# Three of four query and key tiles of a quarter leave VectorE for ScalarE and two strided DMAs each

## The chip, the cores and the metric

One core of a Trainium2 chip runs the whole program in one launch. The metric is the device time of one execution in microseconds, here over three runs. All data is fp32.

## The reference

Three stages follow each other on 64 images of 3x96x96 and 64 texts of 77x256:

```python
h = tokenizer(x)                       # conv 14x14, window attention, class token: 5 tokens of 256 per image
h = concatenate([h, txt], axis=1)      # 64 x 82 x 256
h = h + attention(layernorm(h))        # 16 heads of 16, sine/cosine relative bias
h = h + experts(layernorm(h))          # 8 experts, low rank 64, top 2, gelu
# attention:
#   q, k, v = split(ln(x) @ w_qkv + b_qkv)
#   p = softmax(q @ k.T * 16**-0.5 + rel_bias[i - j])
#   out = (p @ v) @ w_out + b_out
```

## The kernel before

The tokenizer runs first. After it the attention runs as a pipeline written out by hand, one block b (one image, T = 82 tokens) per period, b = 0 to 63. Each engine has its own list of steps for a period, and semaphores join them. GpSimd normalises rows, adds the residual and scatters rows for the experts. In the last blocks the experts' work begins, and it goes on after the loop.

In a period TensorE does, in this order: `scores(b)` (L1443, 32 small matmuls into the four banks `psS`), `weigh(b-2)` (L1464), `turn(b-1, 0)` (L1452, a transpose of the probabilities), where due `xT` (L1409, a transpose of 128 token rows) and `val` (L1430, their values), `turn(b-1, 1)`, where due `project` (L1476, the output projection), `turn(b-1, 2)`, one projection `qk` (L1418), a late step of the tokenizer while there are any, and `turn(b-1, 3)`. All but the scores write into a ring of four banks, `psQ`, in the order of a list `uses`; a use waits until the use four places before it has been read.

Queries and keys are made by quarters of 4 blocks (QT = 328 columns). Quarter q has four tiles: j = 0 and 1 are halves of the queries, j = 2 and 3 halves of the keys. `qk(q, j)` is computed in the period with (b + 1) // 4 + 1 = q and (b + 1) % 4 = j, so tile 0 in period 4k + 3, tiles 1 to 3 in the three periods that follow, and the quarter is used from two periods after tile 3. The tiles go to `qT` and `kT`, two views of `qk_space`, double-buffered by q % 2. Each tile is held twice, for a = 0 and 1. In copy a the partitions of parity a hold the queries (or keys) of 16 columns each; the other partitions hold sine and cosine rows, which carry the relative bias through the same matmul and are equal in every quarter. `scores(b)` waits for tile 3 of its quarter and for both halves of the softmax shift of the block before, since `psS` is single.

VectorE does per period: `shift(b, 0)` and `shift(b, 1)` (each a maximum, L1846, and a subtraction, L1848), in even periods between them `invert` (L1863, the reciprocal of the softmax sums), then statistics for token rows, `read_qk` (L1834: two instructions per tile, `copy = bank * own + add`, one for each a), late tokenizer steps, and in odd periods `divide` (L1874).

ScalarE does `copy_sums` (L1665), four `copy_probT` (L1685), two exponentials (L1677), the evictions `copy_xT`, `copy_val`, `copy_project`, and after the fourth `copy_probT` for 16 row tiles a `split` (L1693).

SP issues nearly all DMAs from one queue. In even periods: `pack` (L1147, after the gathered sums have landed), `send_shares` (L1155, after the reciprocal), `load_values` (L1179), values and output stores, `spread_shares` (L1164, two DMAs, after the shares have landed in DRAM), then `load(b)` (tokens or expert weights). In odd periods `gather_den` (L1142) comes first, after `copy_sums`. `divide` waits for the spread.

Of the kernel before, what the change touches and what calls it, by code (L numbers as in the profile page):

```python
# [35 lines left out]
NEARLY = 2  # L36
QLEAD = 2
# [19 lines left out]
def tokenizer_block(nc, ctx, S, I, R, A, L, big, pout, cout, ident_all, banks):  # L57
    NN = NTOK // 128 * TOPK
    HB = NB // 2
    GROUPS = ((0, 1), (1, 2), (2, 4), (4, 9), (9, 13), (13, 18))  # L60

# [37 lines left out]
    gbq_row = sb("gbq_row", [128, C])  # L99
    pj_row = sb("pj_row", [128, C]); gpj_row = sb("gpj_row", [HB, C])  # L100
# [32 lines left out]
    def sync(sp):  # L133
        sp.dma_start(patches[:, 0, 0:QLEAD, :], I["patches"][:, 0, 0:QLEAD, :]).then_inc(S["lead_in"], 16)
        for k, (lo, hi) in enumerate(GROUPS):
            if k == 2:
                sp.dma_start(ei[:], I["ff_expert_indices"]).then_inc(S["r_in"], 16)
                sp.dma_start(ew[:], I["ff_expert_weights"]).then_inc(S["r_in"], 16)
                sp.dma_start(steps[:], I["steps"]).then_inc(S["r_in"], 16)
                sp.dma_start(upper[:], I["upper"]).then_inc(S["r_in"], 16)  # L140
                sp.dma_start(keep[:], I["keep"]).then_inc(S["r_in"], 16)
            if k == 3:
                sp.dma_start(ident_all[:], I["ident"]).then_inc(S["ident_in"], 16)
                sp.dma_start(cols[:], I["cols"]).then_inc(S["ident_in"], 16)
                sp.dma_start(cls[:], row(I["class_emb"], 128)).then_inc(S["ident_in"], 16)
                sp.dma_start(entry[:], I["entry"]).then_inc(S["r_entry"], 16)
                sp.dma_start(R["list"], I["unfilled"]).then_inc(S["r_entry"], 16)
            if k == 4:
                sp.dma_start(wq[:], I["la_wq"].rearrange("(c p) n -> p c n", p=128)).then_inc(S["law_in"], 16)
                sp.dma_start(wkv[:], I["la_wkv"].rearrange("(c p) n -> p c n", p=128)).then_inc(S["law_in"], 16)  # L150
            if k == 0:
                sp.dma_start(patches[:, 0, QLEAD:5, :], I["patches"][:, 0, QLEAD:5, :]).then_inc(S["img_in0"], 16)
            else:
                sp.dma_start(patches[:, lo:hi, :, :], I["patches"][:, lo:hi, :, :]).then_inc(S["img_in%d" % k], 16)
# [104 lines left out]
    def tensor(te):  # L259
# [5 lines left out]
        def conv(n):  # L265

            if n == 0:
                te.wait_ge(S["ones_set"], 1)
                keep_busy(PS8[0], 9)
                te.wait_ge(S["conv_lead_in"], 16)  # L270
                te.wait_ge(S["lead_in"], 16)
            for k, (lo, hi) in enumerate(GROUPS):
                if n == lo and n > 0:
                    te.wait_ge(S["img_in%d" % k], 16)
            if n >= 2:
                te.wait_ge(S["pe_ready"], n - 1)
            if n == 9:
                te.wait_ge(S["v_read"], NW)
            for q in range(5):
                if n == 0 and q == QLEAD:  # L280
                    te.wait_ge(S["conv_in"], 16)
                    te.wait_ge(S["img_in0"], 16)
                mm = te.matmul(PS8[n % 2][:, 0:C], patches[:, n, q, :], cwT[:, q, :], start=(q == 0), stop=(q == 4))  # L283
            mm.then_inc(S["conv_done"], 1)
# [324 lines left out]
    def vector(v):  # L609
# [252 lines left out]
        for n in range(11, 22):  # L862
# [16 lines left out]
            if n == 15:  # L879
# [36 lines left out]
    return (sync, gpsimd, tensor, scalar, vector), {"early": early, "cwT": cwT, "wq": wq, "wkv": wkv, "gwq": gwq}  # L916
# [32 lines left out]
def attention_space(sb):  # L949
# [5 lines left out]
         "wrel": sb("wrel", [128, 2, 2, 2]), "own": sb("own", [128, 2]), "ownq": sb("ownq", [128, 2]), "bown": sb("bown", [128, 2, 4]),  # L955
# [13 lines left out]
def attention_and_experts(nc, ctx, S, I, R, A, L, W, H, pc, ident_all, out, banks, old):  # L969
# [48 lines left out]
    to_act = ("xT", "val", "project")  # L1018
    by_act = {use: 1 + sum(u[0] in to_act for u in uses[:k]) for k, use in enumerate(uses) if use[0] in to_act}
    by_dve = {use: 1 + sum(u[0] == "qk" for u in uses[:k]) for k, use in enumerate(uses) if use[0] == "qk"}  # L1020
# [9 lines left out]
    mx = sb("mx", [T, 2, 2, 4])  # L1030
    prob_all = sb("prob", [128, 2 * HG * 4 * T])
# [45 lines left out]
    texp = R["tile_expert"]  # L1077

# [18 lines left out]
    def sync(sp):  # L1097
# [68 lines left out]

        def send_values(n):
# [20 lines left out]
        for b in range(-1, NB):  # L1188
# [13 lines left out]
            if b >= 4 and b % 2 == 0:  # L1202
                spread_shares(b // 2 - 2)
            load(b)
# [28 lines left out]
        for n in range(0, NX, 2):  # L1233
            sp.dma_start(yg_two(n), rows[:, n:n + 2, :, :]).then_inc(S["yg_in%d" % (n // 2)], 16)
# [134 lines left out]
    def tensor(te):  # L1369
        def free(use):  # L1370

            k = place[use]
            if k >= RING:
# [3 lines left out]
                elif before[0] == "qk":  # L1377
# [263 lines left out]
    def scalar(act):  # L1641
# [9 lines left out]

        def copy_val(n):
# [103 lines left out]
        for b in range(NB):  # L1756
# [20 lines left out]
            if b >= 1:  # L1777
                copy_probT(b - 1, 3)
            for n in projected(b - 5):
# [27 lines left out]
        for n in range(NX):  # L1807
            if n % 2 == 0:
                act.wait_ge(S["yg_in%d" % (n // 2)], 16)
# [3 lines left out]
    def vector(v):  # L1813
# [148 lines left out]
        for b in range(NB):  # L1962
# [13 lines left out]
            if (b + 1) // 4 + 1 < NQ:  # L1976
# [28 lines left out]
        for n in range(0, NX, 2):  # L2005
            v.wait_ge(S["yg_in%d" % (n // 2)], 16)
# [181 lines left out]
```

## Time and profile before

| | us |
|---|---|
| median of 3 runs (598.92 to 599.81) | 599.6 |
| the profiled execution, its own time | 596.89 |
| its span, first to last instruction | 595.0 |
| PE busy over the span | 545.7 |
| VectorE (DVE) busy | 477.2 |
| ScalarE (ACT) busy | 367.1 |
| GpSimd (POOL) busy | 314.5 |

The span is the profile's own window, some 2 us shorter than the time of the same execution. Matmuls are pipelined and their ends are modelled, so a busy TensorE is not yet one that has no time to give. The time before an instruction is told as idle time of its engine, with what released it. A chain row says what the end of the program was waiting for at that moment, so a duration there is the part that counts, without overlaps.

### The profile page before, as it was taken

To read this page: it belongs to the slowest core of one execution; us is meant where nothing else is said; L and a number is where in the kernel's file an instruction comes from. 1 tells how busy PE (TensorE), PEld (TensorE's weight loads), DVE (VectorE), ACT (ScalarE), POOL (GpSimd) and SP (SyncE) were. 2 spreads that over 40 slices of the span, in tenths; PEclk is the share of its full clock that TensorE was granted. 3 is DMA by queue.
4 is the path that set the end of the run, shared out by engine and by line. 5 is a ranking of instruction groups with operands and counts; after the bars stand their busy time and mean duration, and the time that the engine had idled before them with its cause. 6 is when DMAs were issued, how large, how long until landed. Compare 5 with 4: busy or idle time off the path is not lost.

```text
span 595.0 us, 20410 instructions
## 1 busy us (share of the span) xinstructions
PE 545.7 (92%) x7904; PEld 456.3 (77%) x7904; DVE 477.2 (80%) x967; ACT 367.1 (62%) x793; POOL 314.5 (53%) x401
## 2 busy tenths in 40 slices
PE   9999989989999999999999999999998799999940
PEld 7788867767788778877888788888886678888830
DVE  3666868898999899999999889998887756666617
ACT  1232234156676677777777677677778667777724
POOL 1577773436746688888888524443121244444430
PEclk9999999989999999999999999999999999999975
DMA  8999301422332334666666644333254354545349
GB/s 280 399 326 333 103 10 43 137 76 82 103 87 87 115 125 134 186 200 199 206 206 194 188 137 148 96 119 124 87 144 139 84 131 107 114 117 114 68 140 327
DMA packets 78185, 89.49 MB, mean 150 GB/s; under 512 B 33550, under 2 KB 58638, under 8 KB 77580
## 3 DMA queue, kind: packets, MB, share of 16 engines
q1 hardware_dynamic: 73340, 78.20, 42.9%
q0 software_dynamic: 4464, 9.35, 5.1%
q8 instruction: 64, 1.05, 0.8%
q10 hardware_dynamic: 288, 0.66, 0.3%
q14 instruction: 29, 0.24, 0.1%
HBM read 48.82 MB, written 36.29 MB: 143 GB/s over the span
## 4 chain that ended last, share of the span: by engine, by line
PE 60%; DVE 20%; issue 8%; DMA 5%; ACT 4%; SPq 1%; POOL 1%; DVEq 0%; POOLq 0%; ACTq 0%
PE banks L1452 8%; PE banks L1418 7%; PE banks L1562 7%; PE banks L1464 6%; DVE mx L1846 6%; PE banks L1577 6%; PE banks L1430 5%; PE banks L1476 4%; PE banks L283 3%; PE banks L1443 3%; DVE prob L1848 3%; DVE qk_space L1834 2%; PE banks L323 2%; ACT probT L1685 2%; PE banks L1547 2%
## 5 line engine op out<-in xcount | busy, mean ns | idle before, releaser
L1685 ACT ACTIVATE probT<-banks 82x328 f32<-82x328 f32 x256 | 109.1, 434 | 9.6 <-PE banks L1452 9.3
L1848 DVE TENSOR_TENSOR prob<-banks,mx 82x656 f32<-82x656 f32 x128 | 107.1, 837 | 4.4
L1452 PE MATMUL banks<-ident_all,prob 82*82 82x82 f32 x1024 | 109.6, 237 | 1.1 <-ACT early L1665 0.9
L1452 PEld LDWEIGHTS banks<-ident_all,prob 82*82 82x82 f32 x1024 | 88.1, 120 | 28.2 <-issue 6.7
L1846 DVE TENSOR_REDUCE mx<-banks 82x8 f32<-82x656 f32 x128 | 104.3, 815 | 5.2 <-PE banks L1443 4.0
L1677 ACT ACTIVATE prob<-prob 82x656 f32<-82x656 f32 x128 | 95.5, 746 | 15.8 <-DVE prob L1848 15.1
L1418 PE MATMUL banks<-hT,wqkv 128*128 128x328 f32 (+10 forms) x320 | 80.6, 385 | 0.0
L1296 POOL TENSOR_TENSOR big<-big,gwq 128x256 f32<-128x256 f32 x41 | 30.2, 738 | 88.0 <-ACT gwq L1672 87.5
L1357 POOL DMA_INDIRECT entry_rows<-cwT,slot_entry x39 | 39.7, 1018 | 63.1 <-ACT cwT L1730 57.3
L1665 ACT ACTIVATE early<-banks 128x328 f32<-128x328 f32 x64 | 28.5, 445 | 56.8 <-PE banks L1464 43.8
L1443 PE MATMUL banks<-qk_space 32*82 32x82 f32 x2048 | 53.0, 240 | 7.4 <-DVE prob L1848 5.7
L1892 DVE COPY qk_space<-ex_weights 64x640 f32 x78 | 39.4, 505 | 25.0 <-PE banks L1590 23.8
L1464 PE MATMUL banks<-probT,vv 82*32 82x82 f32 x2048 | 50.1, 238 | 7.5 <-ACT probT L1685 6.5
L1418 PEld LDWEIGHTS banks<-hT,wqkv 128*128 128x128 f32 x320 | 50.3, 191 | 7.6
L1443 PEld LDWEIGHTS banks<-qk_space 32*82 32x82 f32 x2048 | 43.8, 147 | 16.0 <-issue 8.9
L1721 ACT ACTIVATE hT<-banks 128x1024 f32<-128x1024 f32 (+1 forms) x40 | 38.1, 1000 | 21.3 <-PE banks L1562 21.3
L1464 PEld LDWEIGHTS banks<-probT,vv 82*32 82x32 f32 x2048 | 37.8, 110 | 15.5 <-ACT probT L1685 12.1
L1283 POOL TENSOR_SCALAR xh<-big,a_mv,a_rst 128x256 f32<-128x256 f32 x35 | 44.3, 1266 | 6.3 <-PE banks L1409 2.6
L1430 PE MATMUL banks<-wqkv,hT 128*128 128x256 f32 x164 | 43.7, 390 | 0.0
L1476 PE MATMUL banks<-wout,wkv 128*128 128x256 f32 x164 | 43.6, 390 | 0.0
L283 PE MATMUL banks<-cwT,big 128*128 128x256 f32 x180 | 40.5, 381 | 1.8 <-DMA big<-in_patches 1.3
L1562 PE MATMUL banks<-wq,qk_space 64*128 64x128 f32 x624 | 41.1, 278 | 1.1 <-issue 1.1
(275 smaller groups left out, 1011.3 us busy)
## 6 DMA issues: line engine op xcount, KB each, us to landing
vv<-value_rows SPq DMA_DIRECT2D x57, 192.0 KB
value_rows<-vs SPq DMA_DIRECT2D x41, 256.0 KB, 2.9
share<-shares SPq DMA_DIRECT2D x64, 82.0 KB
slot_rows<-xh SPq DMA_DIRECT2D x1, 4992.0 KB, 33.0
fused_rows<-in_txt SPq DMA_DIRECT2D x1, 4928.0 KB
big<-in_patches SPq DMA_DIRECT2D x2, 1600.0 KB, 12.3
out<-big SPq DMA_DIRECT2D x25, 128.0 KB
big<-entry_rows SPq DMA_DIRECT2D x6, 512.0 KB, 6.5
```

The lines of the kernel that those rows point to most:

```text
L283: mm = te.matmul(PS8[n % 2][:, 0:C], patches[:, n, q, :], cwT[:, q, :], start=(q == 0), stop=(q == 4))
L1418: mm = te.matmul(bank(("qk", 4 * q + j))[:, lo:lo + size], wqkv[:, c, 128 * j:128 * j + 128], hT[:, c, a:a + size], start=(c == 0), stop=( ...
L1430: mm = te.matmul(bank(("val", n))[:, 0:C], hT[:, c, a:a + 128], wv[:, c, :], start=(c == 0), stop=(c == 1))
L1443: mm = te.matmul(psS[0:T, g, s:s + T], qT[rows, par, a, t, cols], kT[rows, par, a, t, cols], start=True, stop=True)
L1452: mm = te.transpose(bank(("turn", 4 * b + g))[0:T, s * T:s * T + T], prob[:, b % 2, g, s, :], ident_all[0:T, 0:T])
L1464: mm = te.matmul(bank(("weigh", b))[32 * g:32 * g + 32, lo:lo + T], vv[0:T, b % 4, 8 * t + 2 * g + a, :], probT[:, b % 2, g, 2 * t + a, :] ...
L1476: mm = te.matmul(bank(("project", n))[:, 0:C], attT[:, c, a:a + 128], wout[:, c, :], start=(c == 0), stop=(c == 1))
L1562: mm = te.matmul(psH[:, f // 4, h, f % 4 * 128:f % 4 * 128 + 128], wb[rows, p % 2, f * 128:f * 128 + 128], t1T[rows, p % 2, :], start=True ...
L1677: act.activation(prob[:, b % 2, 2 * half:2 * half + 2, :, :], prob[:, b % 2, 2 * half:2 * half + 2, :, :], ACT.Exp).then_inc(S["prob_ready ...
L1685: act.activation(probT[:, b % 2, g, :, :].rearrange("p s t -> p (s t)"), bank(("turn", 4 * b + g))[0:T, 0:4 * T], ACT.Copy).then_inc(S["pr ...
L1846: v.tensor_reduce(mx[:, half, :, :], s4, X, ALU.max).then_inc(S["max_ready"], 1)
L1848: v.tensor_tensor(prob[:, b % 2, 2 * half:2 * half + 2, :, :], s4, mx[:, half, :, :].unsqueeze(3).to_broadcast([T, 2, 4, T]), ALU.subtract ...
```

## The change

Quarters 0 and 1 stay as they are. From quarter 2 (`QMOVED`) on, tiles 0, 1 and 2 are evicted by ScalarE: one activation of 128x328 with the bias and the scale, into a plain row buffer. SP then places it by two DMAs per tile, each from the 64 partitions of one parity to the same partitions of copy a. The constant partitions of the copies keep what VectorE wrote there for quarters 0 and 1. Tile 3 stays with VectorE. The eviction stands after `copy_probT(b-1, 3)` in ScalarE's list; the placement stands in the next period of SP's list, after `spread_shares` and ahead of `load`. Scores wait for the six placements of their quarter as well. The row buffers lie in tensors of the tokenizer (`red`, `wg1`, `past`), and a few semaphores are shared and renamed, which changes no wait.

```diff
+                v.tensor_scalar(A["qkb"][:, 0:2], cols[:, 20:22], float(HD) ** -0.5, None, ALU.mult)
+                v.tensor_copy(A["qkb"][:, 2:4], cols[:, 22:24])
...
+    QMOVED = 2
+
+    def to_act(use):
+        return use[0] in ("xT", "val", "project") or (use[0] == "qk" and use[1] >= 4 * QMOVED and use[1] % 4 < 3)
...
+    def moved(b):
+        q = (b + 1) // 4 + 1
+        return [(q, (b + 1) % 4)] if ("qk", 4 * q + (b + 1) % 4) in by_act else []
...
+    rows_qk = [old["red"][:].rearrange("p r c -> p (r c)")[:, 0:QT], old["wg1"][:].rearrange("p r c -> p (r c)")[:, 0:QT],
+               old["past"][:].rearrange("p j e -> p (j e)")[:, 0:QT]]
...
+        def send_qk(q, j):
+
+            sp.wait_ge(S["psQ_act"], by_act["qk", 4 * q + j])
+            if j == 0:
+                sp.wait_ge(S["scores_done"], 4 * (q - 1))
+            rows, t = qT if j < 2 else kT, j % 2
+            for a in range(2):
+                sp.dma_start(rows[a:128:2, q % 2, a, t, :], rows_qk[j][a:128:2, :]).then_inc(S["qk_sent%d" % (q % 2)], 16)
+
...
+            for q, j in moved(b - 1):
+                send_qk(q, j)
             load(b)
...
         def scores(b):
 
             te.wait_ge(S["psQ_dve"], by_dve["qk", 4 * (b // 4) + 3])
+            if b // 4 >= QMOVED:
+                te.wait_ge(S["qk_sent%d" % (b // 4 % 2)], 16 * 6 * (b // 8))
...
+        def copy_qk(q, j):
+
+            act.wait_ge(S["qk_done"], 4 * q + j + 1)
+            if j == 0 and q > QMOVED:
+                act.wait_ge(S["qk_sent%d" % ((q - 1) % 2)], 16 * 6 * ((q - 1) // 2))
+            act.activation(rows_qk[j], bank(("qk", 4 * q + j))[:, 0:QT], ACT.Identity, bias=A["qkb"][:, j:j + 1],
+                           scale=float(HD) ** -0.5 if j < 2 else 1.0).then_inc(S["psQ_act"], 1)
...
             if b >= 1:
                 copy_probT(b - 1, 3)
+            for q, j in moved(b):
+                copy_qk(q, j)
...
-            if (b + 1) // 4 + 1 < NQ:
+            if (b + 1) // 4 + 1 < NQ and not moved(b):
                 read_qk((b + 1) // 4 + 1, (b + 1) % 4)
```

## Rows read from the trace of the kernel before

**Rows 1.** Windows: busy us (instructions) per engine, granted clock, DMA share, GB/s

```profile
core 0: us, PE busy (x) PEld busy (x) DVE busy (x) ACT busy (x) POOL busy (x), PEclk, DMA share, GB/s
135.05:440.44 305.39, 297.53 (x5158) 246.26 (x5158) 284.52 (x513) 220.98 (x517) 192.57 (x254) 1.00 0.46 140
265.10:340.57 75.47, 73.54 (x1284) 60.77 (x1283) 70.85 (x129) 57.40 (x134) 63.39 (x82) 1.00 0.65 200
```

**Rows 2.** The page: the chain that ended last, by engine

```profile
PE 60%; DVE 20%; issue 8%; DMA 5%; ACT 4%; SPq 1%; POOL 1%; DVEq 0%; POOLq 0%; ACTq 0%
```

**Rows 3.** The chain in order of time, 240 to 275: start, us, what

```profile
248.81 0.76 PE banks L1443 x32
249.57 0.73 PE banks L1464 x32
250.30 0.41 PE banks L1452 x4
250.71 0.22 PE banks L1409 x2
250.93 0.87 PE banks L1430 x4
...
252.08 0.90 PE banks L1476 x4
...
253.27 1.16 PE banks L1418 x4
...
257.76 0.40 DVE den L1863
```

**Rows 4.** TensorE's groups, 135.04 to 440.43: count, busy, mean ns, idle before

```profile
L1464 PE MATMUL banks<-probT,vv 82*32 82x82 f32 x1792 | 43.9, 238 | 4.1 <-ACT probT L1685 3.2 <-DVE qk_space L1834 0.3
L1430 PE MATMUL banks<-wqkv,hT 128*128 128x256 f32 x144 | 37.4, 382 | 0.0
L1476 PE MATMUL banks<-wout,wkv 128*128 128x256 f32 x132 | 35.3, 390 | 0.0
L1409 PE MATMUL banks<-ident_all,xh 128*128 128x128 f32 x66 | 12.7, 272 | 0.0
```

**Rows 5.** VectorE's groups, 135.04 to 440.43

```profile
L1846 DVE TENSOR_REDUCE mx<-banks 82x8 f32<-82x656 f32 x112 | 91.2, 814 | 1.6 <-PE banks L1443 0.5 <-issue 0.2
L1834 DVE SCALAR_TENSOR_TENSOR qk_space<-banks,own,kadd 128x328 f32<-128x328 f32 x57 | 29.0, 550 | 7.6 <-PE banks L1418 7.5
L1834 DVE SCALAR_TENSOR_TENSOR qk_space<-banks,ownq,qadd 128x328 f32<-128x328 f32 x56 | 28.4, 549 | 5.4 <-PE banks L1418 5.1
```

**Rows 6.** ScalarE's sums copy, 135.04 to 440.43

```profile
L1665 ACT ACTIVATE early<-banks 128x328 f32<-128x328 f32 x56 | 25.0, 446 | 50.1 <-PE banks L1464 39.5 <-DVE wkv L1874 9.3 <-issue 1.3
```

**Rows 7.** Timeline of TensorE: start, us, instruction

```profile
297.38 0.83 PE L1443 MATMUL banks<-qk_space 32*82 32x82 f32 x32
...
361.51 0.83 PE L1443 MATMUL banks<-qk_space 32*82 32x82 f32 x32
```

**Rows 8.** Timeline of SP's queue: start, us on the queue, DMA

```profile
292.76 1.17 SPq L1164 DMA_DIRECT2D share<-shares  x2
294.47 0.56 SPq L1142 DMA_DIRECT2D den<-early  x1
...
299.28 0.53 SPq L1147 DMA_DIRECT2D early<-early  x1
...
325.16 1.16 SPq L1164 DMA_DIRECT2D share<-shares  x2
...
356.93 1.15 SPq L1164 DMA_DIRECT2D share<-shares  x2
```

**Rows 9.** DMA issues, 250 to 300, then 350 to 400: KB, median us to landing

```profile
early<-early SPq DMA_DIRECT2D x5, 82.0 KB, 4.3
...
early<-early SPq DMA_DIRECT2D x5, 82.0 KB, 2.5
```

**Rows 10.** Timeline of VectorE: a division that waited for its spread

```profile
331.19 0.50 DVE L1874 TENSOR_TENSOR wkv<-early,share 128x328 f32<-128x328 f32 x1 [0.70 <-DMA share<-shares]
```

**Rows 11.** Timeline of VectorE in the tokenizer

```profile
94.29 0.22 DVE L887 TENSOR_SCALAR bown<-cols,ownq 128x2 f32<-128x2 f32 x1
94.42 0.22 DVE L888 TENSOR_SCALAR bown<-cols,own 128x2 f32<-128x2 f32 x1
```

More of the change, by code:

```diff
@@ L36 @@
 NEARLY = 2
+GROUPS = ((0, 1), (1, 2), (2, 4), (4, 9), (9, 13), (13, 18))
 QLEAD = 2
@@ L59, in tokenizer_block @@
     HB = NB // 2
-    GROUPS = ((0, 1), (1, 2), (2, 4), (4, 9), (9, 13), (13, 18))
     items = []
@@ L98, in tokenizer_block @@
     bq_row = early[:, 1024:1024 + C]
-    gbq_row = sb("gbq_row", [128, C])
-    pj_row = sb("pj_row", [128, C]); gpj_row = sb("gpj_row", [HB, C])
+    bias_rows = sb("bias_rows", [128, 2, C])
+    gbq_row, pj_row = (bias_rows[:, k, :] for k in range(2))
+    gpj_row = sb("gpj_row", [HB, C])
     cls = sb("cls", [128, C])
@@ L914, in vector @@
             read_quarter(k)
-    return (sync, gpsimd, tensor, scalar, vector), {"early": early, "cwT": cwT, "wq": wq, "wkv": wkv, "gwq": gwq}
+    return (sync, gpsimd, tensor, scalar, vector), {"early": early, "cwT": cwT, "wq": wq, "wkv": wkv, "gwq": gwq, "red": red, "wg1": wg1, "past": past, "bias_rows": bias_rows}
 LATE = ("agg", "aggT", "loutT", "lout", "wpj", "wmod", "gwkv", "gwpj", "gv", "mod_row", "gbv_row", "cls_row", "bkv_row", "xn", "xT", "qv",
@@ L1017, in attention_and_experts, with to_dve @@
     place = {use: k for k, use in enumerate(uses)}
-    to_act = ("xT", "val", "project")
-    by_act = {use: 1 + sum(u[0] in to_act for u in uses[:k]) for k, use in enumerate(uses) if use[0] in to_act}
-    by_dve = {use: 1 + sum(u[0] == "qk" for u in uses[:k]) for k, use in enumerate(uses) if use[0] == "qk"}
+    QMOVED = 2
+    def to_act(use):
+        return use[0] in ("xT", "val", "project") or (use[0] == "qk" and use[1] >= 4 * QMOVED and use[1] % 4 < 3)
+    def to_dve(use):
+        return use[0] == "qk" and not to_act(use)
+    by_act = {use: 1 + sum(to_act(u) for u in uses[:k]) for k, use in enumerate(uses) if to_act(use)}
+    by_dve = {use: 1 + sum(to_dve(u) for u in uses[:k]) for k, use in enumerate(uses) if to_dve(use)}
+    def moved(b):
+        q = (b + 1) // 4 + 1
+        return [(q, (b + 1) % 4)] if ("qk", 4 * q + (b + 1) % 4) in by_act else []
     def sb(name, shape, dt=F32):
@@ L1077, in attention_and_experts, with rows_in @@
     texp = R["tile_expert"]
+    def rows_in(k):
+        return 16 + 16 * (k < len(GROUPS))
     def yg(n, k):
@@ L1233, in sync @@
         for n in range(0, NX, 2):
-            sp.dma_start(yg_two(n), rows[:, n:n + 2, :, :]).then_inc(S["yg_in%d" % (n // 2)], 16)
+            sp.dma_start(yg_two(n), rows[:, n:n + 2, :, :]).then_inc(S["piece_in%d" % (n // 2)], 16)
         for n in range(0, NX, 2):
@@ L1376, in free @@
                     te.wait_ge(S["sums_copied"], before[1] + 1)
-                elif before[0] == "qk":
+                elif before in by_dve:
                     te.wait_ge(S["psQ_dve"], by_dve[before])
```

14 lines of the change are left out of this document (7 added, 7 removed).

## The prediction

> **What bounds the kernel now.** I read the stage table first [rows 1]. The change acts on the blocks b = 3 to 57, in the stretch from 135.05 to 440.44 us, which starts and ends with a group of scores and holds 56 periods in 305.4 us. There TensorE is busy for 297.5 us, VectorE for 284.5, ScalarE for 221.0, at full granted clock and with the DMA engines 46% busy. Two engines near the top: the question is which of them sets the period. The chain of waits over the whole run [rows 2] gives 60% to PE and 20% to DVE, so both do, in turn. Seen in order of time [rows 3], a period is normally TensorE's own list: scores 0.76, weighing 0.73, four turns 0.41 and three times 0.28 (such a turn is what lies between the pieces at 252.08 and 253.27), the query or key projection 1.16, and where they are due a token turn 0.22, values 0.87, the output projection 0.90. Where VectorE comes late, the chain passes through its work instead, as in the reciprocal of the denominators at 257.76.
>
> How much do these latenesses cost? I price TensorE's list for the 56 periods [rows 3, 4]. The fixed part is 2.72 + 1.15 = 3.87, times 56 = 216.7 us. L1430 x144 is 36 value tiles at 0.87 = 31.3, L1476 x132 is 33 projections at 0.90 = 29.7, L1409 x66 is 33 token turns at 0.22 = 7.3. Twenty projections split at the ring's end cost 0.17 more each, 3.4, and the tokenizer's late matmuls are seven blocks of the size of a value tile, 0.87 each = 6.1, and a few small ones, 6.2 together. Sum 294.6. The stretch takes 305.4, so 10.8 us are not TensorE's own work. That is the most a lighter VectorE can give; the busy time it saves is far larger and mostly worthless.
>
> **The change part by part.** *VectorE.* Three of four tiles of quarters 2 to 15 leave it: 42 tiles, 84 instructions of 0.55 us [rows 5], 46 us of busy time before overlap. Its load falls from 93% to about 78% of the stretch, under TensorE's 97%. Scores to scores the fixed chain is the scores' 0.8, two maxima of 0.81 and two subtractions of about the same [rows 5], in even periods the reciprocal of 0.4 [rows 3] between them: 4.2 to 4.7 us with hand-overs, below TensorE's lightest period of 3.87 + 0.90 = 4.77. So late starts of VectorE should vanish. Not all of the 10.8 us: TensorE waits 3.2 us before L1464 for ScalarE's probabilities [rows 4], and most of these waits come in even periods, after the reciprocal and also where VectorE had been idle. I leave 3.3 us standing. Gain 7.5 us, bounds 5 and 10.8.
>
> *ScalarE.* It gets 42 activations of 128x328 from a bank. L1665 is that shape and takes 0.446 us [rows 6]; 42 x 0.446 = 19 us. The Trainium skill, "ScalarE: Activation LUTs", section "What ACT_TABLE_LOAD costs", gives about 93 ns more for a bias that is a pointer; no row here shows this form on this shape, and it would make 23 us. The new copy stands after the fourth probability copy and before the sums copy, L1665, which idles 50.1 us before its 56 runs, 39.5 of them for TensorE's weighing [rows 6]: 0.7 us each time, more than the 0.45. In the sixteen periods where the split copy stands there too, the cover is about used up. The bank is wanted again only four uses later, after the next weighing and turn. Cost 0; with no cover it is 19 us.
>
> *SP and the DMAs.* 84 placements, each from 64 partitions to 64 alternate ones, 82 KB. The pack L1147 is the same in kind and size: 0.53 us on SP's queue [rows 8], landing in 2.5 us where the queue is quiet, in 4.3 us in the 250 to 300 us window [rows 9]. The 7 MB are no burden as bytes. The moment counts. The third tile's pair goes out in the even period 4k+2, behind SP's spread L1164, which waits for the shares' round trip, and the scores of period 4k+4 need it. Quiet quarter: spread 356.93 plus 1.15, second placement from 358.7, plus 2.5 lands at 361.2; scores are due at 361.51 [rows 7, 8]. It fits by 0.3. Loaded quarter: spread 292.76 plus 1.17, second placement from 294.55, plus 4.3 is 298.85; due at 297.38 [rows 7, 8]. 1.5 us late, or 0.3 early with the quiet landing. Queued behind this wait on TensorE are the scores and all that follows, so the wait is paid in full. Four quarters, every fourth period from 276 to 341, lie in the loaded stretch from 265.10 to 340.57, which has 65% DMA share [rows 1]. Bounds 0 and 1.5 us each there, 0 and 0.5 for the other ten; I take 0.9 and 0, that is 3.6 us (0 to 11), nearer to the loaded landing because the spread itself needed about 6.0 us there (SP issues at 325.16, the division ends its wait for it at 331.19) [rows 8, 10].
>
> The Trainium skill, "DMA: Bandwidth & Descriptors", section "Anatomy of one DMA", gives (for the GpSimd path) about 2.0 us and the bytes over 436 GB/s: an estimate of 2.2 us for 82 KB. The quiet row is near it, the loaded row is not, and by the page nothing would be late and the forecast 3.6 us lower. The measurement decides.
>
> Second, SP itself. The placements take 1.1 us of its queue in three periods of four. In even periods they stand before the next block's loads and before the gather of the denominators L1142, which then waits its turn: L1142 starts at 294.47 and its pack, which needs it landed, at 299.28 [rows 8]. The reciprocal, which needs it too, is due after that period's scores, first maximum and first subtraction: 297.38 [rows 7] plus 0.83, 0.81 and about 0.83, at 299.9. The slack there is 0.6 us; delayed by 1.1, it comes 0.5 late, between the two halves of the softmax. Eight gathers in the loaded stretch by 0.5 are 4 us, the upper bound; most even periods have more on TensorE's list than VectorE's 4.7, which hides it: I take 0.7 us in all, lower bound 0. The spread is not preceded by a placement in its own period.
>
> *TensorE.* No matmul changes. Scores get one more wait, 52 times. Weighing, at 249.57, stands behind three waits and starts as the scores end (248.81 plus 0.76) [rows 3]: a wait that is already met costs nothing that shows, and I take 0. I bound it by 0.04 us, a few times the rounding of these pieces: 2 us in all. *Front.* Two more tiny VectorE operations beside the four of L887 and L888, of 0.22 us each and partly overlapping [rows 11], in a stretch where VectorE's row of work leads to the class and patch rows that the first token loads wait for: 0.25 us, bounds 0 and 0.44. Merged tensors, renamed and shared semaphores: nothing issued, nothing waited for longer. GpSimd: nothing.
>
> Sum: 7.5 - 3.6 - 0.7 - 0.25 = 2.95 us. The profiled execution took 596.89 us (span 595.0), so 593.9 after; the median of the runs is 599.6, 2.7 above it, and moves by the same: 596.6 us.
>
> **The rivals.** *All hidden.* The placements land in time everywhere and the gathers keep their slack: 7.5 - 0.25, or up to 9 with all waits gone: 590.6 to 594, about 592.3. For it: 10 of 14 quarters fit as they stand. Against it: the loaded landings. *The landing becomes the bound* (the other side). The third tile arrives late in most quarters, because its descriptors stand behind the spread and the value loads. From 0.5 us per quarter (7.25 over 14) it eats the gain, at 1 us it is 14 - 7.25 = 7 slower: about 603 to 606. For it: the spread's 6.0 us, and the quiet fit of only 0.3, which shrinks as the two periods before it get shorter by some 0.2 each. Against it: the quiet pack lands in 2.5 us at most quarters, and VectorE's earlier reciprocal moves the spread forward too. The Trainium skill, same page, section "Queues, rings and completion order", says that on each DMA engine the descriptors of one issuing queue are consumed in ring order; by that rule placements follow the spread on every engine, which is this rival's mechanism. *The change buys nothing.* TensorE was the bound, and periods where VectorE came late are paid back in the next, so little is recovered, or recovery and new waits cancel: 598.4 to 600.8. For it: VectorE already idles 12.6 us before its reads of the projections in this stretch [rows 5]. Against it: the 10.8 us are net of any paying back.
>
> **How the numbers follow.** Forecast case (part of the gain kept, 594 to 598.4) 0.38; all hidden 0.20; nothing 0.18; landing binds 0.24. Bounds of sign are 0.2% or 1.2 us, about what a measurement of this kernel can tell from no change. Faster 0.58, same 0.18, slower 0.24. The range 591 to 603 leaves out the best of the second case and the worst of the last, about 0.15 together. The forecast case alone: 594 to 598.4.
>
> **What would show it.** In the profile after: VectorE's busy time over the run down by 40 to 46 us with 84 fewer L1834 instructions; ScalarE up by 19 to 23 and its idle before the sums copy down by as much; the wait of scores for VectorE's subtraction gone from nearly all periods; at scores of every fourth period a wait for a DMA into qk_space, near 1 us between 270 and 345 us and absent elsewhere; L1142 issued about 1 us later in relation to its period; division waits for share a little more often. Wrong would make it: such waits in the quiet quarters (slower), the reciprocal waiting for den in many periods, ScalarE's copy pushing the turns, or scores starting later at every block by the extra wait.

## The result, and the profile after

The median went from 599.26 us (598.74 to 599.81) to 608.82 us (607.02 to 609.68), four runs each: 1.0146 times the time before, 95% interval 1.0107 to 1.0184. The prediction was 596.6 us: the change makes the kernel 9.6 us slower, beyond the range. Each ratio, here and below, leaves out executions more than 1.5% above the fastest of their kernel: none or one of ten as a rule, but three of ten where the placements stand at the head. The profiled execution after took 607.02 us, span 605.2; the one before 596.89 and 595.0 [rows 1 to 11].

The page of the kernel after: busy time of each engine, the chain by engine, and the three groups that answer to [rows 4 to 6]:

```profile
PE 550.7 (91%) x7904; PEld 461.6 (76%) x7904; DVE 442.8 (73%) x885; ACT 384.2 (63%) x835; POOL 314.9 (52%) x401
PE 75%; DVE 7%; issue 5%; POOL 4%; ACT 3%; DMA 3%; SPq 2%; DVEq 0%; POOLq 0%; ACTq 0%
L1886 DVE TENSOR_REDUCE mx<-banks 82x8 f32<-82x656 f32 x128 | 104.6, 817 | 44.2 <-PE banks L1473 43.6
L1473 PE MATMUL banks<-qk_space 32*82 32x82 f32 x2048 | 53.0, 240 | 15.9 <-issue 10.7
L1703 ACT ACTIVATE early<-banks 128x328 f32<-128x328 f32 x64 | 28.4, 444 | 43.8 <-PE banks L1494 39.6
```

VectorE left the chain (20% of it before [rows 2], 7% now), as the change intends, and now it waits for the scores. The scores have 10.7 us of idle time that no engine released. The waits from 130 to 460 us say who waits (us in total, times, longest); first TensorE and VectorE, with ScalarE's copy of a quarter's first tile:

```profile
DVE mx L1886 <- PE banks L1473: 39.3, 36, 3.1
DVE wkv L1914 <- DMA share<-shares: 14.1, 10, 2.1
PE banks L1473 <- issue: 10.7, 8, 2.8
ACT red L1687 <- DMA qk_space<-past: 5.5, 5, 2.4
PE banks L1473 <- DVE prob L1888: 2.8, 4, 1.2
PE banks L1494 <- ACT probT L1723: 1.1, 4, 0.4
```

ScalarE's copy for the next quarter waits on the same counter as the scores, and there the profile names the releaser: the placement of the third tile, `past`. The timeline shows both engines released by it, in the loaded stretch (start, length, engine, line, idle before):

```profile
320.86 0.53 ACT L1687 ACTIVATE red<-banks,qkb 128x328 f32<-128x328 f32 x1 [2.36 <-DMA qk_space<-past]
```

```profile
317.57 0.45 PE L1482 MATMUL banks<-ident_all,prob 82*82 82x82 f32 x4
320.87 0.83 PE L1473 MATMUL banks<-qk_space 32*82 32x82 f32 x32 [2.85 <-issue]
365.85 0.83 PE L1473 MATMUL banks<-qk_space 32*82 32x82 f32 x32 [1.93 <-issue]
```

The eight waits are at 208.37, 275.01, 297.32, 320.87, 365.85, 389.46, 410.57 and 453.89 us, all at the first scores of a quarter. Three, 5.35 us together, lie between 265 and 341 us; five, 5.36 us, lie outside.

SP's queue around the quiet quarter's wait at 365.85:

```profile
355.12 2.21 SPq L1191 DMA_DIRECT2D qk_space<-wg  x2
357.38 0.59 SPq L1164 DMA_DIRECT2D early<-early  x1
358.07 0.54 SPq L1172 DMA_DIRECT2D shares<-den  x1
360.27 1.18 SPq L1181 DMA_DIRECT2D share<-shares  x2
361.51 1.42 SPq L1191 DMA_DIRECT2D qk_space<-past  x2
362.97 0.58 SPq L1159 DMA_DIRECT2D den<-early  x1
```

and the reciprocal that L1172 sends, from VectorE's timeline:

```profile
356.68 0.40 DVE L1903 RECIPROCAL den<-den 64x41 f32<-64x41 f32 x1
```

The reciprocal is ready at 357.08, but its shares go out at 358.07: SP was busy with the second tile's placement until 357.33 and then issued the pack. All that follows is late: spread 360.27, third tile's placement 361.51, the gather behind it 362.97. The scores would have started at 365.85 - 1.93 = 363.92.

Last, the windows (length, then busy us of PE, PEld, DVE, ACT and POOL with counts, the granted clock, DMA share, GB/s), scores to scores: the two periods around the wait at 320.87, the one after it, and the period after the wait at 365.85:

```profile
313.17:320.87 7.70, 4.85 (x89) 3.91 (x89) 5.77 (x10) 4.44 (x11) 6.90 (x9) 1.00 0.63 199
320.87:327.50 6.63, 6.63 (x90) 5.38 (x90) 3.71 (x6) 4.44 (x10) 5.57 (x8) 0.74 0.79 249
327.50:332.52 5.02, 5.02 (x93) 4.12 (x91) 4.02 (x7) 4.45 (x11) 0.88 (x2) 1.00 0.70 204
365.85:372.43 6.58, 6.58 (x94) 5.68 (x94) 3.52 (x5) 3.68 (x9) 1.68 (x3) 0.74 0.29 87
```

The period that follows each of these two waits has no idle time, yet takes 6.6 us, at a granted clock of 0.74: part of it ran at 1.2 GHz instead of 2.4. In the kernel before, the same two periods take 5.04 us each at full clock, also without idle time; the second of them:

```profile
361.51:366.55 5.04, 5.04 (x97) 4.50 (x95) 4.97 (x10) 3.53 (x10) 3.54 (x5) 1.00 0.08 26
```

So the wait of 2.85 us cost 1.6 more, and the one of 1.93 us cost 1.5 more.

**Where the time went.** I price TensorE's list for each of the 57 periods from the scores of block 3 to those of block 60 (299.6 us in all, as the prediction does) and take it from the period's length:

| | 57 periods, us | beyond TensorE's list |
|---|---|---|
| before | 310.2 | 10.7 |
| after | 320.0 | 20.3 |
| after: last period of eight quarters | | 12.7 |
| after: slow clock behind two waits | | 3.1 |
| after: all 47 others | | 4.5 |

The stretch grew by 9.8 us, which is nearly the whole loss of this execution (10.1). The last periods of the eight late quarters and the clock hold 15.8 us, of which 10.7 are the scores' waits themselves and 3.1 the clock; elsewhere the excess fell. The split depends little on how the list is priced: with the shortest length that each period has in any of the runs (301.7 us in all) in its place, the excess is 8.5 before and 18.2 after, of which 11.9 lie in those eight periods and 3.3 behind the two waits.

### The profile page after: what moved, and what is told of

Its sections match the earlier page's. It is cut to its first block, busy times and chain, and to the rows that moved or that the text cites. A ratio compares the mean times of both kernels' runs of the same rounds, so it can differ in the third digit from the quotient of the medians.

```text
span 605.2 us, 20439 instructions
## 1 busy us (share of the span) xinstructions
PE 550.7 (91%) x7904; PEld 461.6 (76%) x7904; DVE 442.8 (73%) x885; ACT 384.2 (63%) x835; POOL 314.9 (52%) x401
## 4 chain that ended last, share of the span: by engine, by line
PE 75%; DVE 7%; issue 5%; POOL 4%; ACT 3%; DMA 3%; SPq 2%; DVEq 0%; POOLq 0%; ACTq 0%
PE banks L1482 10%; PE banks L1446 9%; PE banks L1592 7%; PE banks L1494 6%; PE banks L1473 6%; PE banks L1607 6%; PE banks L1506 5%; PE banks L1458 5%; PE banks L283 5%; PE banks L323 3%; PE banks L331 2%; PE banks L1577 2%; DVE mx L1886 2%; DMA big<-in_patches 1%; PE banks L1620 1%
## 5 line engine op out<-in xcount | busy, mean ns | idle before, releaser
L1482 PE MATMUL banks<-ident_all,prob 82*82 82x82 f32 x1024 | 111.2, 240 | 0.9 <-ACT early L1703 0.9
L1482 PEld LDWEIGHTS banks<-ident_all,prob 82*82 82x82 f32 x1024 | 89.6, 122 | 28.3 <-issue 6.9
L1715 ACT ACTIVATE prob<-prob 82x656 f32<-82x656 f32 x128 | 95.3, 745 | 10.8 <-DVE prob L1888 10.5
L1473 PE MATMUL banks<-qk_space 32*82 32x82 f32 x2048 | 53.0, 240 | 15.9 <-issue 10.7
L1311 POOL TENSOR_SCALAR xh<-big,a_mv,a_rst 128x256 f32<-128x256 f32 x35 | 42.9, 1226 | 6.0 <-PE banks L1437 2.3
L1592 PE MATMUL banks<-wq,qk_space 64*128 64x128 f32 x624 | 42.8, 285 | 0.6 <-issue 0.6
L1592 PEld LDWEIGHTS banks<-wq,qk_space 64*128 64x128 f32 x624 | 39.4, 195 | 4.5 <-issue 4.5
```

Source lines behind the costliest of these rows:

```text
L1311: pool.tensor_scalar(xh[:, n % 3, :], H[:, n, :], mv[:, n % 4, 0:1], rst[:, n % 4:n % 4 + 1], ALU.subtract, ALU.mult).then_inc(S["xh_ready ...
L1473: mm = te.matmul(psS[0:T, g, s:s + T], qT[rows, par, a, t, cols], kT[rows, par, a, t, cols], start=True, stop=True)
L1482: mm = te.transpose(bank(("turn", 4 * b + g))[0:T, s * T:s * T + T], prob[:, b % 2, g, s, :], ident_all[0:T, 0:T])
L1592: mm = te.matmul(psH[:, f // 4, h, f % 4 * 128:f % 4 * 128 + 128], wb[rows, p % 2, f * 128:f * 128 + 128], t1T[rows, p % 2, :], start=True ...
L1715: act.activation(prob[:, b % 2, 2 * half:2 * half + 2, :, :], prob[:, b % 2, 2 * half:2 * half + 2, :, :], ACT.Exp).then_inc(S["prob_ready ...
```

## The experiments

The theory was that the third tile's deadline takes the time (the transfer lands late, and TensorE waits). The rivals: that the placements cost SP time and delay the softmax's own round trips (gather, pack, shares, spread), whoever waits for the tiles; that the bytes slow other transfers; that ScalarE's 42 copies cost something. Each ratio is against the kernel before on the same chip, with its 95% interval. Diffs are against the kernel after unless said otherwise; where fewer placements are made, the counts that the scores and ScalarE wait for are lowered to match, which the diffs here don't show.

**No placement.** The 84 placements and the two waits for them are gone; the scores of quarters 2 to 15 read old values in three of four tiles.

```
-            for q, j in moved(b - 1):
-                send_qk(q, j)
...
-            if b // 4 >= QMOVED:
-                te.wait_ge(S["qk_sent%d" % (b // 4 % 2)], 16 * 6 * (b // 8))
...
-            if j == 0 and q > QMOVED:
-                act.wait_ge(S["qk_sent%d" % ((q - 1) % 2)], 16 * 6 * ((q - 1) // 2))
```

> The changed kernel without its 84 placements and without the waits for them; ScalarE still evicts the 42 tiles, VectorE still keeps the fourth, and the scores read what quarters 0 and 1 left (so the output is another). It prices the relief of VectorE and the load on ScalarE with no DMA in it. If the relief is worth what the prediction said (7.5 us less 0.25 us) it runs 6 to 9 us faster than before, near 592. If ScalarE's 42 evictions cost something, it comes out between 594 and 599. If the relief is worthless, since TensorE sets the period, it runs like before.

Measured 0.9923 [0.9885, 0.9962], median 594.74 us. VectorE's relief is real: 4.6 us net of anything that ScalarE's 42 copies cost, and the 57 periods take 305.5 us, 4.7 less than before. That the copies cost nothing shows in TensorE's waits for ScalarE's probabilities, which fell (first row, the kernel before; second, this one):

```profile
PE banks L1464 <- ACT probT L1685: 4.8, 20, 0.7
```

```profile
PE banks L1490 <- ACT probT L1717: 2.8, 9, 0.7
```

The whole loss comes from the placements: 1.0146 against 0.9923 is 13.4 us.

**Placed into a scratch tensor.** Same DMAs at the same place of SP's list, to rows that nobody reads, so the scores don't wait for them; old values as above. SP itself waits before the third tile until the first one has landed.

```
+    room_qk = sb("room_qk", [128, QT])
+    scratch = [room_qk[:], old["bias_rows"][:].rearrange("p k c -> p (k c)")[:, 0:QT], room_qk[:]]
...
+            if j == 2:
+                sp.wait_ge(S["qk_sent%d" % (q % 2)], 16 * (6 * (q // 2 - 1) + 4))
...
+                sp.dma_start(scratch[j][a:128:2, :], rows_qk[j][a:128:2, :]).then_inc(S["qk_sent%d" % (q % 2)], 16)
```

> The changed kernel with the same 84 placements at the same places of SP's list, but into tensors that nobody reads, and with no wait of the scores for them (output is another). ScalarE's wait before it refills the first row buffer stays. Theory landing (the loss is the scores' wait for the third tile): most of it is gone, 593 to 597 us. Theory traffic (SP's longer list and the added bytes delay the gathers, spreads and loads, whoever waits for the tiles): as slow as the changed kernel, 605 to 609.

Measured 1.0062 [1.0018, 1.0105], median 603.48 us. With the deadline gone, some 5 us come back and some 8 remain. The deadline is thus not the whole loss. In its waits the delay sits at the spread:

```profile
DVE wkv L1915 <- DMA share<-shares: 20.7, 16, 3.1
```

against 2.5 us in 4 waits in the kernel before and 8.5 in 10 without placements.

**Same DMAs with sources that never change, and with 16 of 328 columns.** Also to scratch, both without the waits of scores and ScalarE, which are SP's here.

```
-                sp.dma_start(rows[a:128:2, q % 2, a, t, :], rows_qk[j][a:128:2, :]).then_inc(S["qk_sent%d" % (q % 2)], 16)
+                sp.dma_start(scratch[j][a:128:2, 0:328], A["qadd"][:].rearrange("p a t n -> p (a t n)")[a:128:2, 0:328]).then_inc(S["qk_sent%d" % (q % 2)], 16)
...
+                sp.dma_start(scratch[j][a:128:2, 0:16], A["qadd"][:].rearrange("p a t n -> p (a t n)")[a:128:2, 0:16]).then_inc(S["qk_sent%d" % (q % 2)], 16)
```

> The 84 placements at their places in SP's list and of their full size, but from a constant tensor into tensors that nobody reads. Neither the scores nor ScalarE wait for them; only SP does, for older ones (output is another: queries and keys stay those of quarters 0 and 1). Against the run without placements (0.992 of before) it is the price of SP's longer list and of the bytes alone. Theory deadline (only waits for the tiles cost): 0.990 to 0.997. Theory traffic (the spread of the shares and the loads come later in the loaded stretch): 1.000 to 1.006, with the divisions waiting for share as in the scratch run (20.7 us).

> As the static run, with 16 columns instead of 328 in each placement: the same number of DMAs and of pieces, 5% of the bytes (output is another). If SP's time per DMA is what delays the rest, it is as slow as the static run. If the bytes in the DMA engines are, it comes down to the run without placements, 0.990 to 0.995.

Measured 1.0046 [1.0012, 1.0079] and 1.0058 [1.0023, 1.0093]. A twentieth of the bytes buys nothing back: the cost goes with the number of DMAs, not with what they carry. SP's issues show it; first the kernel after, then the 16 columns (ns, shortest, median, longest of one):

```profile
L1191 SPq DMA_DIRECT2D qk_space<-red x28: 521/557/1216, 145.3 to 439.4; - x28
L1191 SPq DMA_DIRECT2D qk_space<-wg x28: 483/596/1572, 148.3 to 445.2; - x28
L1191 SPq DMA_DIRECT2D qk_space<-past x28: 516/572/1479, 155.5 to 450.5; - x28
```

```profile
L1196 SPq DMA_DIRECT2D room_qk<-qadd x56: 517/558/1584, 143.9 to 440.2; - x56
L1196 SPq DMA_DIRECT2D bias_rows<-qadd x28: 483/596/1538, 146.8 to 434.8; - x28
```

SP's queue, summed over its timeline from 130 to 450 us, is busy for about 154 us before, 208 after and 216 with 16 columns: from 48% of the time to about 66%.

**The placements at the head of the period.** Real placements with their waits, but ahead of pack, shares, spread and value loads instead of behind them.

```
+            for q, j in moved(b - 1):
+                send_qk(q, j)
...
-            for q, j in moved(b - 1):
-                send_qk(q, j)
```

> All three tiles as in the changed kernel, but SP issues the placement at the head of its period instead of after the spread, so it need not wait for the shares' round trip: about 5 us earlier for the third tile. Theory landing: the waits for qk_space vanish and it runs at 592 to 597 us. Theory traffic: the packs and gathers stand behind the placements now and the time stays at 604 to 610 us.

Measured 0.9962 [0.9914, 1.0011], median of all ten executions 599.17 us: the same 84 DMAs, and 1.6% (by the medians) to 1.8% (by the ratios) less time than the kernel after. It is not shown to be faster than the kernel before, whose median here is 599.05. The scores no longer wait for a placement at all; the spread's wait is longer, and it passes on to ScalarE's sums copy, which needs the buffer that the division reads:

```profile
DVE wkv L1914 <- DMA share<-shares: 24.3, 19, 3.7
ACT early L1703 <- DVE wkv L1914: 8.2, 8, 3.4
PE banks L1482 <- ACT early L1703: 2.5, 1, 2.5
```

Part of that is not the number of DMAs. At the head, SP itself stands still until ScalarE has evicted the tile, and the pack stands behind it: 24.7 us in 13 waits for the first tile, and 18.0 in 9 for the third. In the kernel after, its waits at the placements are 5.6 us in all.

```profile
SPq L1191 <- ACT red L1687: 24.7, 13, 3.4
```

So the position decides most, and those waits of VectorE are mostly hidden: 24.3 us of them go with a time not above the one before.

**Only two tiles moved** (56 placements; VectorE keeps the third).

```
-        ... (use[0] == "qk" and use[1] >= 4 * QMOVED and use[1] % 4 < 3)
+        ... (use[0] == "qk" and use[1] >= 4 * QMOVED and use[1] % 4 < 2)
```

> Only tiles 0 and 1 of a quarter leave VectorE; tiles 2 and 3 stay. The second tile's placement has three periods before its scores, the third tile had two. Theory landing: no scores wait for a DMA, two thirds of the relief are kept, 593 to 597 us. Theory traffic: two thirds of the loss stay, 604 to 606 us.

Measured 0.9999 [0.9959, 1.0039]. Without the late tile the loss is gone, and without its relief so is the gain. No scores waited for a placement. In its profiled execution two periods in a row, of blocks 28 and 29, hold 6.5 of the 14.1 us of excess, the second at the lower clock.

**Only one tile moved** (28 placements): the second one, where it stood.

```
+        ... (use[0] == "qk" and use[1] >= 4 * QMOVED and use[1] % 4 == 1)
```

> Only tile 1 of a quarter leaves VectorE. It is evicted in an even period, where VectorE has the reciprocal as well, and placed in an odd one, three periods ahead of its scores: 28 placements instead of 84. Theory SP's list: its 17 us of SP time fit into the odd periods and a good part of the relief stays: 0.993 to 0.997. If relief goes by the number of tiles moved, it is 0.998 to 1.000.

Measured 0.9978 [0.9949, 1.0008]. The interval holds both expectations. Then **only the third tile**, late as in the change, and the same at the head of the period:

> Only tile 2 leaves VectorE, placed behind the spread of the even period as in the changed kernel: 28 placements, as many as in the run with tile 1 alone (0.998 of before), but with the late deadline. Theory deadline: scores wait for a DMA every fourth period also with a third of the placements, above all near 270 to 345 us, and the time is 1.000 to 1.008. Theory number of placements: as with tile 1 alone, 0.995 to 1.000, and no such waits.

> Tile 2 alone, placed at the head of the even period. Against the run before it only the moment differs. Theory deadline: no scores wait and 0.994 to 0.999. If the moment does not matter, the two runs agree.

Measured 1.0024 [0.9992, 1.0057] late, 0.9977 [0.9939, 1.0014] at the head. The order is what the deadline would make of it, but the intervals overlap. With 28 placements in all the late tile's waits are shorter: the first scores of ten quarters start late, by 6.4 us together, the longest 1.3, and none at the head. (The view of waits puts three of the ten, 3.3 us, down to VectorE's eviction of another quarter's first tile, for which these scores don't wait.) So the third tile alone makes over half of the 10.7 us, and the rest needs the other placements on SP's queue too.

The pair settles how the landing depends on the moment. It is the same DMA of the same tile, here from 355 to 425 us, at a DMA share of 0.40 and 0.41; first behind the spread, then at the head (from the start of the issue to the landing, where the profile has it):

```profile
DMA to landing us min/median/max: 3.2/3.4/3.4
```

```profile
DMA to landing us min/median/max: 1.9/2.0/2.4
```

**Half of each placement**: only one of the two DMAs of a tile, so 42 for all three tiles, late as in the change. Half of the moved rows keep old values.

```
-            for a in range(2):
+            for a in range(1):
```

> The changed kernel with one of the two placements of each tile left out (copy a = 1 keeps the values of quarters 0 and 1, so the output is another): 42 DMAs, 41 KB fewer per pair stay out, all waits kept. Theory SP's list and deadline: the third tile leaves SP 0.6 us sooner and the list is 26 us shorter, so about half of the loss against the run without placements goes: 0.998 to 1.005, where the changed kernel has 1.015. If the waits are set by the landing alone, it stays at 1.010 to 1.015.

Measured 0.9954 [0.9921, 0.9987]. With the three tiles, the three moments and the deadline all kept, half the DMAs turn 1.5% slower into 0.5% faster; the scores' waits fall to 3.6 us in 6, the longest 1.0. SP's waits for ScalarE's evictions are all kept here too, so they are not what makes the change slow; what the run halves is the issues and the bytes at once, and the 16 columns above tell these apart only for the part without deadline.

**The placements on ScalarE's queue**, issued after the first of its four probability copies of the next period.

```
+            for a in range(2):
+                act.dma_start(rows[a:128:2, q % 2, a, t, :], rows_qk[j][a:128:2, :]).then_inc(S["qk_sent%d" % (q % 2)], 16)
```

> All 84 placements, issued by ScalarE after its first probability copy of the next period, none by SP. Theory SP's list: SP's gathers, packs and spreads go back to their times without placements; what the issuing costs ScalarE decides, at 0.6 us each it is 1.3 us in three periods of four on an engine that is busy for 80%: 0.995 to 1.010. Theory bytes or DMA engines: the divisions go on waiting for share as long as before (about 14 to 20 us).

Measured 1.012 [1.0069, 1.017]. SP is freed: about 155 us busy, and its gather waits again for ScalarE's sums copy instead of coming late (first row, the kernel after; second, this one):

```profile
SPq L1159 <- ACT early L1703: 6.9, 7, 4.0
```

```profile
SPq L1159 <- ACT early L1701: 31.4, 22, 4.0
```

No scores wait for a placement either. But ScalarE issues 84 DMAs between its copies, and now TensorE waits for those:

```profile
PE banks L1483 <- ACT probT L1721: 5.2, 17, 0.8
PE banks L1435 <- ACT hT L1668: 4.9, 17, 1.3
```

**The weights of the next stage loaded half as often**, so that fewer loads lie between the quarter's DMAs from block 25 on; with the kernel after, and with the placements at the head.

```
-            if 25 <= b < 25 + 2 * NE:
-                e = (b - 25) // 2
+            if 25 <= b < 25 + 4 * NE and b % 2 == 1:
+                e = (b - 25) // 4
```

> The changed kernel with the same slower loading of expert weights. If the late landing of the third tile is a matter of the loaded stretch alone, no scores wait and the time is 0.993 to 0.997. If the spread ahead of it and SP's own round trip make it late anyway, waits of 1 to 2 us stay in the quiet quarters and move into those from 345 to 420 us: 1.005 to 1.015.

> The placements at the head of SP's period, and the sixteen loads of expert weights spread over every second period from 25 to 55 instead of every period from 25 to 40. If the remaining loss of the head version (0.996, one gap of 2.7 us near 290 us) is the loaded stretch, it goes, and the time is 0.988 to 0.993 of before. If it is SP's list, it stays at 0.996.

Measured 1.009 [1.0043, 1.0137] and 0.9999 [0.9967, 1.003]. The first is some third less slow than the change, but the intervals overlap. Its scores still wait for 8.3 us, in 5 quarters: 4.0 and 1.4 before 281 us, 0.7, 0.4 and 1.9 after 367 us, and none in between, where the change had its longest. The second does nothing for the head version. Neither has a partner of the kernel before with slow loads alone, so I read only this from them: the loads are not the main cause.

**The first two tiles' placements together, in the odd period** behind SP's other work, the third tile's at the head of the even period (against the head version).

```
             for q, j in moved(b - 1):
-                send_qk(q, j)
+                if j == 2:
+                    send_qk(q, j)
...
+            for q, j in moved(b - 1):
+                if j == 1:
+                    send_qk(q, 0)
+                    send_qk(q, 1)
```

> Same 84 placements, other moments: those of tiles 0 and 1 together in the odd period, where SP has no round trip, those of tile 2 at the head of the even period, before the pack. Theory deadline plus SP's list: no scores wait for a DMA, and the spreads of half the even periods are no longer pushed: 0.992 to 0.997 of before. If only the number of DMAs on SP counts, wherever they stand, it is 0.998 to 1.005 like the static run.

Measured 1.0174 [1.0117, 1.023]: the worst of all. Four placements end the odd period and two begin the next, so six stand between a gather and its pack, where the round trip to the division passes:

```profile
DVE wkv L1919 <- DMA share<-shares: 31.9, 17, 4.7
ACT early L1708 <- DVE wkv L1919: 17.6, 9, 3.3
PE banks L1487 <- ACT early L1708: 3.6, 2, 1.9
PE banks L1511 <- DVE wkv L1919: 3.6, 2, 2.5
```

Same DMAs, same bytes, none of them with a scores' wait, and 2.1% above the head version. It is the cost of the delayed round trips, which reach TensorE through the sums copy and the output projection (last two rows), and of the clock behind them: the period with the longest of these waits ran at a granted clock of 0.69, the one after the last at 0.55.

**The kernel after once more**, to see which of its waits return.

> The changed kernel itself, on the same chip as the two before. Expected 1.011 to 1.018 of before, with waits of scores for a DMA of about 1 to 3 us each at seven to nine of fourteen quarters and granted clock at half in the periods after the longest of them.

Measured 1.0139 [1.0068, 1.021]. Excess 19.9 us, again in the last periods of quarters; 8.5 us of scores' waits in 9, and two periods behind them at the lower clock (a third follows after the stretch). The first scores of the blocks 28, 32, 44 and 60 wait again, 0.86, 1.89, 1.81 and 1.80 us (1.06, 1.44, 1.93 and 1.45 in the first profile); those of block 36 wait 0.54, where it was 2.85. So the place of the loss repeats and the size of a single wait does not. Single slow issues have a part in the size: before the wait of 2.85 the placement landed after 3.9 us, and its issue alone took 1.48 of them, where the median is 0.57.

## Why the prediction was wrong, point by point

**What bounds the kernel: right.** TensorE's list, 299.6 us for 57 periods, and 10.7 us of lateness on it. This is an upper reading: the pieces that the prediction prints add up to 3.90 us per period and not 3.87, which would leave 9.1 of its 10.8, and the shortest period lengths of all runs leave 8.5.

**The relief of VectorE: right in kind, a third too large.** 7.5 us was taken (5 to 10.8); without placements the periods shrink by 4.7 us (310.2 to 305.5) and the run by 4.6. VectorE's busy time from 130 to 445 us:

```profile
130.00:445.00 315.00, 302.27 (x5186) 250.17 (x5175) 250.64 (x431) 239.96 (x562) 193.71 (x255) 0.99 0.51 157
```

250.6 us after, 292.3 before: the 42 us forecast are there. The scores' wait for its subtraction is down to 2.8 us in 4 (4.7 in 10 before).

**ScalarE at 0: right**, by the run without placements. The copy takes 0.52 to 0.53 us, where the sum had 0.446 from the neighbour L1665. By the Trainium skill, "ScalarE: Activation LUTs", section "What ACT_TABLE_LOAD costs", a bias that is a pointer adds about 93 ns, an estimate of 0.54 with this row; the trace is near it. It changes nothing: it is covered.

**The landing of the third tile: this term failed.** 3.6 us were taken, 0.9 for each of four loaded quarters and nothing for ten others. Measured: 10.7 us of waits and 12.7 of excess, in eight quarters, five of them outside the loaded stretch. For the quiet quarter the working can be set against the trace piece by piece. The prediction had the second `past` DMA start 358.7, 2.8 us before the scores are due, and land in 2.5: 0.3 to spare. In the trace it starts at 362.1, 1.8 us before they are due (363.92), and lands at 365.84, 3.7 us later: 1.0 lost at the start, 1.2 in the landing, and the wait is 1.93.

In the loaded quarter at 320.87 it is the start alone: 317.0, just 1.0 before the scores are due at 318.0, while the landing of 3.9 us is within the 4.3 taken. Chance has a share in both: the second tile's first issue at 355.12 took 1.57 us, 1.0 over the median, as much as the quiet quarter's start slipped. In the repeat of the kernel the same placement starts 2.4 us before the scores are due, and they still wait 1.8, since it lands after 4.2. The late landing behind the spread is the part that both profiles share.

So both stamps of the sum were wrong, and mostly for one reason. They came from SP's list of the kernel before, whose pack, shares and spread go out when their data is there. With placements in three periods of four these go out when SP is free, and the third tile stands behind the last of them. Its landing in a quiet moment was read from the pack, which in the kernel before stands some 2 us apart from the transfers ahead of it; the placement follows a spread of the same size at once. The pair with the third tile alone shows the difference: 3.4 us behind the spread, 2.0 at the head. By the Trainium skill, "DMA: Bandwidth & Descriptors", section "Queues, rings and completion order", the descriptors of one issuing queue are consumed in ring order on each DMA engine, and the trace agrees with it, though it doesn't tell the order in the ring from engines that are merely shared.

**Gathers and SP's queue: this term was too small.** 0.7 us (0 to 4) stood there for 84 more DMAs. To scratch, with no deadline, they cost 0.0062 + 0.0077, about 1.4% or 8 us, when they stand late. By the runs this is the largest miss of the sum. What the prediction priced was one gather against one reciprocal. What moved was the whole round trip: the division's waits for `share` grew from 2.5 us in 4 to 14.1 in 10, and 47.9 us of SP's waits for the reciprocal (68.9 before) say how much of its slack is gone. "The spread is not preceded by a placement in its own period" was true and no comfort, since the pack before it is. At the head of the period the same 84 DMAs cost 0.4% over none (0.7% by the medians of all executions): the cost depends on what stands behind them.

**The slow clock after a long wait: missing.** No term was made for it. It is 3.1 us in the periods of this execution, 1.6 and 1.5 behind two waits.

**The sum again, by the runs:** 4.6 - 5.0 (the deadline with its clock, after against scratch) - 8.3 (the placements without deadline, scratch against none) = -8.7 us, where the prediction had 7.5 - 3.6 - 0.7 - 0.25. It fits the measured ratio by construction and says only how large each miss is.

**Extra waits of scores and the front: no sign of either.** Inside the quarters the scores start as before, and the scores of block 3 come at 133.92 us, at 135.05 before.

**The rival.** "The landing becomes the bound" had 0.24 and 603 to 606 us, and it named the mechanism, the placement behind the spread. The result lies above it: it had no slow clock and no late round trips.

What stays open is how the 13.4 us divide between deadline and count. The runs give about 5 for the deadline with its clock (after against scratch) and 8 for the count, but the two are not additive: half the DMAs, with the deadline kept, cost only 2 us more than none. Nor is it shown why the scratch runs are worse than the head version, whose division waits are as long. No version beats the kernel before with all its work in place: the head version, the one tile and the third tile at the head are at 0.996 to 0.998, and two tiles at 1.000, all with intervals that hold 1.

## What to carry to other kernels

Count a DMA on the issuing engine, not only on the wires: here some 0.6 us of queue each, with 16 columns as with 328, and price it against whatever small round trip stands behind it on that queue. When a change adds issues to a queue, don't take stamps for the new work from the old trace of that queue; shift the old ones first, then see whether a slack of a few tenths is left. A transfer with a deadline goes ahead of the list, and transfers that somebody else must wait for are not put in front of a round trip in a bunch.

## What the runs showed of the hardware

- TensorE's granted clock fell to the lower level after waits of 1.93 and 2.85 us in otherwise full periods, and the next list of some 5 us took 1.5 and 1.6 us longer: the 1.93 us wait cost 3.5 in all. The length of the wait alone doesn't decide. Waits of 1.06, 1.44 and 1.15 us (at 275.01, 297.32 and 389.46) were followed by full speed, the one of 1.45 us at 453.89, with another of 1.15 at the scores before it, by a period at 0.68:

```profile
297.32:302.50 5.18, 5.18 (x108) 4.63 (x112) 4.36 (x9) 4.11 (x10) 4.57 (x7) 1.00 0.72 217
453.89:459.19 5.30, 5.30 (x84) 4.48 (x84) 3.52 (x5) 2.65 (x6) 0.40 (x1) 0.68 0.51 142
```

  And in the head version TensorE waited 2.47 us in the middle of a period, with no loss of clock, in the rest of it or in the next:

```profile
290.07 0.46 PE L1482 MATMUL banks<-ident_all,prob 82*82 82x82 f32 x4 [2.47 <-ACT early L1703]
293.14:298.20 5.06, 4.98 (x95) 4.43 (x94) 4.91 (x9) 3.58 (x10) 4.16 (x6) 1.00 0.73 214
```

- Executions of one and the same kernel differ by this clock. Of the kernel before, in the comparisons above, the fastest took 595.45 us at a mean granted clock of 0.982 and one of the slowest 604.56 at 0.961. For the 16 columns it is 596.59 at 0.977 to 605.2 at 0.969. One profile is a sample: effects of 0.5% need the repeated runs.
- A strided transfer of 82 KB within SBUF landed 2.0 us after the start of its issue by SP at the head of the period, and 3.4 us after it right behind the spread's two of that size (medians, DMA share 0.4).
- SP needs as long to issue a DMA of 16 columns as one of 328: 0.56 us in the median for both, with single ones up to 1.6 us in both.
- Sources that are being written or not, full or thin, made no difference that can be measured (1.0062, 1.0046, 1.0058).
